# Two transformer layers in one hand-scheduled kernel: first x by tiles, another order in the opening, GpSimd's pieces ahead of its scaling, the last additions on another engine

## The reference

```python
x = x + attention(_layernorm(x), weight_qkv, weight_proj)   # 16 heads of 128, 4 groups of k and v, causal
x = x + ternary_ffn(_layernorm(x), weight, bias, gamma, beta)
x = x + linear_attention(_layernorm(x), W_in, b_in, W_out, b_out)
x = x + gated_ffn(_layernorm(x), wq_gate, s_gate, wq_up, s_up, wq_down, s_down)

# attention, the part that the opening of the change touches
scores = jnp.einsum('bsgqd,btgd->bgqst', q, k) * scale
scores = jnp.where(causal, scores, jnp.finfo(scores.dtype).min)
attn = jax.nn.softmax(scores, axis=-1)
out = jnp.einsum('bgqst,btgd->bsgqd', attn, v).reshape(b, s, NH * D)
y = jnp.einsum('bse,he->bsh', out, weight_proj)

# gated_ffn, the part that the end of the change touches
gate, up = silu(_qlinear(x, wq_gate, s_gate)), _qlinear(x, wq_up, s_up)
y = _qlinear(gate * up, wq_down, s_down)                    # W = (wq - 128) * s
```

## Time and profile before

| what | us |
|---|---|
| median of 3 runs | 589.16 (586.92 to 590.02) |
| the profiled execution | 586.79 |
| its span, first to last instruction | 584.9 |
| granted TensorE clock over the span | 0.998 of full |
| TensorE busy | 568.9 (97%) |
| VectorE, ScalarE, GpSimd busy | 477.4, 371.8, 221.4 |

### The profile page before, as it was taken

The page is one execution under the profiler, slowest core; times in us unless marked ns, Lnnn a source line. Parts: engine busy times, 40 slices in busy tenths (PEclk is TensorE's granted clock), DMA queues, the critical chain, the costliest instruction groups (busy, mean ns, idle before and its releaser), DMA issues.

```text
span 584.9 us, 12978 instructions
## 1 busy us (share of the span) xinstructions
PE 568.9 (97%) x4180; PEld 535.1 (91%) x4180; DVE 477.4 (82%) x1467; ACT 371.8 (64%) x1043; POOL 221.4 (38%) x325
## 2 busy tenths in 40 slices
PE   7999999999999999999999999999999999899995
PEld 7899999999999999999999999999998988788884
DVE  4789779778967897797789778877887989778885
ACT  5786557656765756576556657657887756554552
POOL 3666223223323332332233233323447778513220
PEclk9999999999999999999999999999999999999999
DMA  8802400000000000000000000000000000001011
GB/s 313 299 2 101 126 2 2 1 1 0 0 0 0 0 0 0 0 0 0 0 0 0 0 0 0 0 0 1 1 1 1 1 2 1 2 0 37 18 33 60
DMA packets 9136, 14.71 MB, mean 25 GB/s; under 512 B 1552, under 2 KB 6672, under 8 KB 9104
## 3 DMA queue, kind: packets, MB, share of 16 engines
q1 hardware_dynamic: 9104, 14.30, 7.0%
HBM read 12.20 MB, written 2.10 MB: 24 GB/s over the span
## 4 chain that ended last, share of the span: by engine, by line
PE 84%; DVE 7%; POOL 3%; ACT 2%; issue 2%; DMA 0%; POOLq 0%; DVEq 0%
PE bank L629 68%; PE bank L715 5%; PE bank L729 5%; PE bank L732 2%; PE bank L639 2%; PE bank L824 1%; ACT prob L1099 1%; DVE pT L1710 1%; DVE prob L1501 1%; DVE raw L1694 1%; DVE prob L1703 1%; DVE prob L1479 1%; POOL qkv L464 1%; DMA x<-in_x 0%; PE bank L893 0%
## 5 line engine op out<-in xcount | busy, mean ns | idle before, releaser
L508 POOL TENSOR_SCALAR prob<-prob,rowinv 128x128 f32<-128x128 f32 (+1 forms) x128 | 96.9, 769 | 275.5 <-DVE rowinv L1495 275.5
L629 PE MATMUL bank<-xT,big 128*128 128x256 f32 x984 | 129.3, 283 | 0.1
L629 PEld LDWEIGHTS bank<-xT,big 128*128 128x128 f32 x984 | 123.4, 192 | 1.0 <-issue 0.2
L1099 ACT ACTIVATE prob<-prob,negmax 128x128 f32<-128x128 f32 (+1 forms) x256 | 112.8, 445 | 7.8 <-DVE negmax L1479 7.8
L629 PE MATMUL bank<-wp,oT 128*128 128x256 f32 x768 | 102.3, 283 | 0.0
L629 PEld LDWEIGHTS bank<-wp,oT 128*128 128x128 f32 x768 | 96.9, 190 | 0.7
L1061 ACT ACTIVATE qT<-bank 128x512 fp32r<-128x512 f32 x68 | 40.6, 598 | 76.8 <-PE bank L629 76.8
L629 PE MATMUL bank<-pT,v 128*128 128x512 f32 (+1 forms) x384 | 79.9, 343 | 0.2
L629 PEld LDWEIGHTS bank<-pT,v 128*128 128x128 f32 x384 | 63.1, 189 | 9.9 <-issue 0.7
L1433 DVE TENSOR_TENSOR pT<-bank,pT 128x512 fp32r<-128x512 f32 (+1 forms) x128 | 65.2, 551 | 2.4 <-ACT pT L1061 2.3
L1061 ACT ACTIVATE pT<-bank 128x512 fp32r<-128x512 f32 (+1 forms) x128 | 55.2, 484 | 12.0 <-PE bank L729 9.5
(11 more groups left out here) (165 smaller groups left out, 973.0 us busy)
## 6 DMA issues: line engine op xcount, KB each, us to landing
x<-in_x SPq DMA_DIRECT2D x8, 256.0 KB, 7.9
raw<-in_wq SPq DMA_DIRECT2D x4, 512.0 KB, 8.2
raw<-in_wp SPq DMA_DIRECT2D x4, 512.0 KB, 8.2
out<-x SPq DMA_DIRECT2D x7, 256.0 KB, 2.1
raw<-in_w_gu SPq DMA_DIRECT2D x2, 640.0 KB, 5.2
raw<-in_w_in SPq DMA_DIRECT2D x1, 768.0 KB, 4.5
raw<-in_w_down SPq DMA_DIRECT2D x1, 640.0 KB, 7.1
raw<-in_wk SPq DMA_DIRECT2D x1, 512.0 KB, 3.8
```

Source lines behind the costliest of these rows:

```text
L508: m = pool.tensor_scalar(prob[:, j % 2, 0, a:b], prob[:, j % 2, 0, a:b], rowinv[:, j % 2, r:r + 1], None, ALU.mult)
L629: m = pe.matmul(out, lhs(a), rhs(b), start=first and i == 0, stop=last and i == len(passes) - 1, skip_group_check=True)
L1099: m = act.activation(prob[:, j % 2, i, a:b], prob[:, j % 2, i, a:b], ACT.Exp, scale=-1.0, bias=negmax[:, 2 * i + r:2 * i + r + 1], accum_o ...
```

## The change

The first x comes in two transfers, one for each of its tiles; VectorE takes the statistics of each tile when it lands and signals each normalised tile by itself, and TensorE transposes tile by tile. ScalarE makes the first q copy ahead of the second late chunk instead of behind it. GpSimd does its weight pieces ahead of its scaling, in the opening and in the iterations of batch 0. ScalarE and VectorE have another order in iteration 0 of batch 0, and VectorE scales ahead of the row maxima in iterations 1 to 4. At the end TensorE alternates the two halves of the last down products, and the sum for sequence 6 moves from VectorE to GpSimd.

```diff
--- before.py
+++ after.py
@@ -173,6 +173,8 @@
         s_x = [sem(f"x_landed{b}") for b in range(NB)]
+        s_x0 = [sem(f"first_x_landed{t}") for t in range(ST)]
+        s_xn0 = sem("first_xn_tile_ready")
         s_raw = [sem(f"raw_landed{c}") for c in range(10)]
         s_const = sem("constants_made")
         s_wsplit = sem("early_weights_split")
@@ -380,7 +382,8 @@
         @block.sync
         def _(sp):
-            sp.dma_start(x[:, 0:ST, :], x_v[0]).then_inc(s_x[0], 16)
+            for t in range(ST):
+                sp.dma_start(x[:, t:t + 1, :], x_v[0][:, t:t + 1]).then_inc(s_x0[t], 16)
             for n, c in enumerate(CHUNKS):
                 if n >= NRAW:
@@ -413,10 +416,10 @@
                 sp.dma_start(wd[half * HLAST:(half + 1) * HLAST, HT - 1, :], wd_in[(HT - 1) * P:HID, :]).then_inc(s_rawl[3], 16)
             for b in range(NB - 1):
-                sp.wait_ge(*((s_ga, b + 3) if b < NB - 2 else (s_gl, 1)))
+                sp.wait_ge(s_ga, b + 3)
                 sp.dma_start(out_v[b], x[:, ST * b:ST * (b + 1), :]).then_inc(s_out, 16)
             for t in range(ST):
-                sp.wait_ge(s_gl, t + 2)
+                sp.wait_ge(s_gl, t + 1)
                 sp.dma_start(out_v[NB - 1][:, t:t + 1], x[:, ST * (NB - 1) + t:ST * (NB - 1) + t + 1, :]).then_inc(s_out, 16)
             sp.wait_ge(s_out, 16 * (NB + 1))
@@ -532,6 +535,8 @@
             def batch(n, last):
                 for j in range(J):
+                    if isinstance(n, int) and n == 0 and j + 4 < len(LATE):
+                        late_lo(j + 4)
                     if j < J - 2 or not last:
                         normalise(*ahead(n, j, 2))
                     if not (isinstance(n, int) and n == 0):
@@ -553,8 +558,6 @@
                             gated_weights_lo(GU1, 0)
                     if j == J - 1 and not last and not (isinstance(n, int) and n == 0):
                         linear_scale(n - 1)
-                    if isinstance(n, int) and n == 0 and j + 4 < len(LATE):
-                        late_lo(j + 4)
             pool.wait_ge(s_var, 1)
             pool.tensor_tensor(rstd[:, :], variance[:, :], exponent[:, 0:ST], ALU.pow).then_inc(s_rs, 1)
@@ -562,8 +565,8 @@
             late_lo(1)
             late_lo(2)
             normalise(0, 0)
+            late_lo(3)
             normalise(0, 1)
-            late_lo(3)
             batch(0, False)
             pool.wait_ge(s_tab, 16 * 6)
             with pool.Fori(1, NB - 1) as n:
@@ -622,6 +625,10 @@
             with pool.Fori(1, NB // 2 - 1) as m:
                 gated(m, False, False)
             gated(NB // 2 - 1, False, True)
+            b = NB - 2
+            pool.wait_ge(s_gsc, b + 1)
+            xs = x[:, ST * b:ST * (b + 1), :]
+            pool.tensor_tensor(xs, xs, scaled[0][:, :, :], ALU.add).then_inc(s_ga, 1)
         def mm3(pe, out, lhs, rhs, first, last, passes=PASSES):
@@ -1010,7 +1017,11 @@
             pe.wait_ge(s_const, 4)
             keep_busy(20)
-            x_transpose(0)
+            for t in range(ST):
+                pe.wait_ge(s_xn0, t + 1)
+                for k in range(KT):
+                    m = pe.transpose(bY[:, k * S + t * P:k * S + (t + 1) * P], xn[:, t, k * P:(k + 1) * P], ident[:])
+            m.then_inc(s_xTp, 1)
             keep_busy(8)
             first_k()
             first_q()
@@ -1042,8 +1053,8 @@
                 with pe.Fori(1, NB // 2 - 1) as m:
                     gated(m, False, False, weight_parts)
                 gated(NB // 2 - 1, False, True, weight_parts)
-                for half in range(2):
-                    for i in (HT - 2, HT - 1):
+                for i in (HT - 2, HT - 1):
+                    for half in range(2):
                         down_project(NB // 2 - 1, i, weight_parts, half)
@@ -1108,7 +1119,11 @@
                         pT_hi(n, j)
                     if first:
                         v_hi(n, 1)
+                        late_hi(4)
                         q_hi(n, 3)
+                        o_hi(n, 0)
+                        exps(n, 2)
+                        pT_hi(n, 1)
                     if last:
                         if j == 0:
                             subtract_zero_point(GU0, 0)
@@ -1122,10 +1137,8 @@
                             subtract_zero_point(GU1, 0)
                         if j == 4:
                             gated_weights_hi(GU1, 0)
-                    if isinstance(n, int) and n == 0 and j + 4 < len(LATE):
+                    if isinstance(n, int) and n == 0 and 0 < j < len(LATE) - 4:
                         late_hi(j + 4)
-                    if first:
-                        pT_hi(n, 1)
                     if j == 1 and isinstance(n, int) and n == 0:
                         act.wait_ge(s_rawt, 16)
                         act.activation(abs_w, raw_t, ACT.Abs, accum_out=abs_sum[:, 0:1]).then_inc(s_abs, 1)
@@ -1167,9 +1180,9 @@
                             linear_k(0, 1)
                     if j == J - 1:
                         o_hi(n, j)
-                    if j < J - 3 or not last:
+                    if (j < J - 3 or not last) and not first:
                         exps(*ahead(n, j, 2))
-                    if j < J - 3 or j < J - 1 and not last:
+                    if (j < J - 3 or j < J - 1 and not last) and not first:
                         o_hi(n, j)
                 if not last:
                     v_hi(n + 1, 0)
@@ -1374,8 +1387,8 @@
             early(1, 1)
             k_hi(0, 0)
             late_hi(0)
+            q_hi(0, 0)
             late_hi(1)
-            q_hi(0, 0)
             late_hi(2)
             k_hi(0, 1)
             q_hi(0, 1)
@@ -1513,14 +1526,19 @@
                     if not (isinstance(n, int) and n == 0 and j == 1):
                         pT_lo(n, j, 0)
                         pT_lo(n, j, 1)
+                    opening = isinstance(n, int) and n == 0 and j < 5
                     if first:
                         v_lo(n, 1)
-                        q_lo(n, 3)
+                    if opening and not first:
+                        normalise(n, j + 1)
                     if j < J - 2 or not last:
                         row_max(*ahead(n, j, 2))
-                        if not first:
+                        if not opening:
                             normalise(*ahead(n, j, 1))
                     if first:
+                        q_lo(n, 3)
+                        o_lo(n, 0)
+                        invert_sums(n, 2)
                         pT_lo(n, 1, 0)
                         pT_lo(n, 1, 1)
                     if j == 0 and not first:
@@ -1845,11 +1863,21 @@
             bG, bU, bD = (bS0, bT0), (bS1, bT1), (bQ, bO)
             dve.wait_ge(s_const, 4)
-            dve.wait_ge(s_x[0], 16)
-            ln_moments(0, 0)
+            for t in range(ST):
+                dve.wait_ge(s_x0[t], 16)
+                m = dve.bn_stats(stats[:, t, :], x_tile(0, t))
+            m.then_inc(s_st, 1)
+            dve.wait_ge(s_st, 1)
+            for t in range(ST):
+                m = dve.bn_aggr(moments[:, t, :], stats[:, t, :])
+            m.then_inc(s_mo, 1)
             dve.wait_ge(s_mo, 1)
             dve.tensor_scalar(variance[:, :], moments[:, :, 1], 1.0, EPS, ALU.mult, ALU.add).then_inc(s_var, 1)
-            x_apply(0)
+            dve.wait_ge(s_rs, 1)
+            for t in range(ST):
+                dve.tensor_scalar(xn[:, t, :], x_tile(0, t), moments[:, t, 0:1], rstd[:, t:t + 1], ALU.subtract,
+                                  ALU.mult).then_inc(s_xn0, 1)
+            dve.sem_inc(s_xn, 1)
             early(0, 0)
             early(0, 1)
             x_lo(0)
@@ -1896,11 +1924,7 @@
             with dve.Fori(1, NB // 2 - 1) as m:
                 gated(m, False, False)
             gated(NB // 2 - 1, False, True)
-            b = NB - 2
-            scale_down(b, 0)
-            dve.wait_ge(s_gsc, b + 1)
-            xs = x[:, ST * b:ST * (b + 1), :]
-            dve.tensor_tensor(xs, xs, scaled[0][:, :, :], ALU.add).then_inc(s_gl, 1)
+            scale_down(NB - 2, 0)
             b = NB - 1
             dve.wait_ge(s_gd, b + 1)
             dve.wait_ge(s_ga, b + 1)
```

## The result

The median fell from 587.25 us (10 executions, 585.3 to 590.02) to **584.3 us** (10 executions, 582.26 to 584.65). The ratio is 0.9935, 95% interval [0.9915, 0.9955]: faster by 0.65%, just over what a measurement of this kernel can tell. The profiled execution took 584.11 (span 582.3) against 586.79 (span 584.9), so **2.68 us less, where the working had summed to 2.7**. What failed isn't the sum but what it was added to; that is settled further down. That the two agree to 0.02 is luck in part: the last sum ends 2.98 us earlier, and 0.4 of it is given back behind it, where the stores land (3.7 us from the last sum to the end of the span before, 4.1 after), which the working hadn't treated.

What follows compares the result with a forecast made beforehand. TensorE is busy nearly all the span, so only its waits can be won, 3.7 us in an early ScalarE, VectorE and GpSimd relay. 0.8 + 2.1 - 0.2 = 2.7 us, off the 589.16 median: 586.5, range 584.9 to 589.1.

Steps and rivals of the forecast that it cites:

- Part 1: Opening, first x by tiles: first products 0.3 us earlier, bounds 0 and 0.3, floored by dummy transposes ending at 6.24.
- Part 2: Opening, q copy ahead of a weight piece: 0.35 us carried to the second pair's exponentials, bounds 0 and 0.9.
- Rival D: Opening's wins eaten by k's late copy, TensorE 0 to 0.3 ahead at 28.50, the 2.1 stand: 587.3 us, chance 0.12.
- Part 3: Iteration 0, row maxima ahead of the q residual: scores of 28.50 come 0.8 us earlier, the carried 0.35 included.
- Part 4: Behind the scores of 28.50: VectorE's scaling and GpSimd's weight pieces no longer meet, 2.1 us of stall goes.
- Part 5: End: VectorE's first sum waits for GpSimd's 512-wide sum, 0.2 us lost, bounds -0.65 and +0.5.
- Rival C: End runs without collision and the third weight copy's data was early: 0.85 + 0.4 more won, 585.2 us, chance 0.09.
- A: Opening: VectorE's scaling meets GpSimd's piece once, 2.0 to 2.4 us lost, 588.7 us, chance 0.23.
- B: Opening: the same meeting in iterations 1 and 2 alike, 1.5 us slower, 590.7 us, chance 0.06.

Runs made afterwards that it cites:

- a_old_end: Kernel after with the end put back as it was (VectorE doing the 512-wide sum): 583.77 us, ratio 0.9925 to the kernel before.
- a_psum_end: Kernel after with VectorE's last products written to PSUM, so its last sums have one SBUF operand: 584.17 us, ratio 0.9954 to the kernel before.
- p4_both: Kernel before with GpSimd's weight pieces ahead of its scaling and VectorE's scaling ahead of the row maxima: 588.53 us, ratio 1.0013.
- p3_iteration0: Kernel before with only the new order of ScalarE and VectorE in iteration 0: 587.49 us, ratio 1.0008.
- p1_tiles: Kernel before with only the first x in two transfers and handled by tiles: 586.73 us, ratio 0.9989.
- p5_end: Kernel before with only the new end (GpSimd adds sequence 6, TensorE alternates the halves): 587.37 us, ratio 0.9996.
- p4b_vector: Kernel before with only VectorE's scaling ahead of the row maxima in iterations 1 to 4, GpSimd's order unchanged: 588.53 us, ratio 1.0012.
- b_fill: Kernel before with sixteen dummy transposes in TensorE's 1.8 us wait ahead of the gated block: 586.87 us, ratio 1.0001.
- b_xlo: Kernel before with VectorE's low part of the gated block's first x moved ahead of its last linear step: 585.79 us, ratio 0.9973.
- p4a_gpsimd: Kernel before with only GpSimd's weight pieces ahead of its scaling, VectorE's scaling still behind the row maxima: 587.55 us, ratio 1.0006.

## Why the prediction was wrong

**The anchor failed, not the sum.** The step reads: "The median of the runs shown is 589.16, 2.4 above it; against that the forecast is 586.5". The sum's own reference, 586.79, gives "584.1 for it", and the profiled execution took 584.11, the median 584.3. The three executions shown were 586.92, 589.16 and 590.02. In the 112 executions above such times as the upper two lie in the third group, that of the fallen clock, which held 34 of 112; the profiled one, with no fall in its trace, lay in the second. So I added a change worked out for the second group to a median that happened to fall in the third. With seven more executions the median is 587.25, and 587.25 - 2.7 is 584.55, within 0.3 of what came. The warning was on the table: a spread of 3.1 us among three executions, against a profile at the lowest of them.

**The sum's parts missed both ways and cancelled.** What came is 1.2 instead of 0.8 at the scores of 28.50, 1.9 instead of 2.1 behind them, -0.1 instead of -0.2 at the end, and -0.4 where the stores land, for which there was no term.

**Why the ratio says 3.8 us and the medians 2.95.** Of the ten executions beside the kernel after, three are of the third group (589.16, 589.91, 590.02), 2.0 to 2.8 us above the second group's 587.2: 0.75 us on the mean. None of the kernel after's ten is. How much of that is luck is open: of 31 executions of the kernel after and its two versions with that wait left in (a_old_end, a_psum_end) three had a clock of 0.991 to 0.994 and were over 586.5; of the kernel before about one in three. What in the change makes the falls rarer wasn't found; p4_both had more of them, not fewer: eight of its ten executions had a clock of 0.993 or less, of the kernel before 10 of 112, of p3_iteration0 two of ten.

**Part 1**: 0.17 came instead of 0.3, since the floor moved (dummy transposes to 6.59 by the timeline, not 6.24); p1_tiles showed 0.6 where the clock rose early. The bounds of 0 and 0.3 were too narrow: they held the floor fixed.

**Part 2**: I carried 0.35; alone it gave 0.56. The reason given for cutting it, that k's copy might not come earlier, fell: it came 0.19 earlier, and the third chunk's data was there. Rival D had that cause and fell with it.

**Part 3** was 0.8 at the scores of 28.50 with parts 1 and 2 in, and 1.2 came: 0.47 for the part alone (0.4 forecast), 0.57 from part 2, and the rest from part 1.

**Part 4** was 2.1 behind those scores, and 3.09 - 1.2 = 1.9 came; alone it gave 1.6. The mechanism, two engines taking turns at a port in an order set by margins of 0.1 to 0.3 us, is shown from both sides: with both halves the pairs take 0.54, with one half 2.48. Parts alone give 0.6 + 0.56 + 0.94 + 1.6 = 3.7 where the whole gave 3.1. Most of the difference is part 1, whose 0.6 came with the early clock; with the 0.17 of the kernel after they give 3.3. That the 0.2 left is parts 3 and 4 shortening the same pairs is likely and not shown.

**Part 5**: a loss of 0.2 was forecast with the sum blocked until GpSimd is done. Blocked it was. The loss is 0.1 at the last sum, in the kernel after and in p5_end alike; the median of a_old_end says 0.5, which one comparison can't tell from 0.1. Rival C's collision-free end didn't happen; its early third chunk did, and that was the smaller half of it.

**A and B** didn't happen, but only starts that lie 0.1 to 0.3 us apart separate p4b_vector, where they did, from the kernel that was measured.

## What to carry to other kernels

Anchor a sum to the same kind of execution as the profile it came from: where the executions fall into groups and a profile shows one of them, a median of three may be of another group, and the difference (here 2.4 us) can equal the change. Where two engines share a port, moving one engine's instruction moves the meeting; both orders have to be moved, and the margin between the starts read off the timeline. And fill or remove a wait of TensorE of 1 to 2 us that stands alone in a busy stretch: it may cost more than its length in some executions.

## What the runs showed of the hardware

- **The granted clock can fall behind a wait of 1.8 us**, from 1 to half (2.4 to 1.2 GHz), for 3.4 or 6.8 us, in some executions of one program and not in others. In the five profiles a fall cost 1.6 to 3.3 us at the first scaled product of the last sequences, less what the openings differ. The Trainium skill, "TensorE: Matmul & The Clock Gate", section "HAM oscillation — how this bites in real kernels", looks for this only behind longer waits; by that rule none of the falls here should have come, and the runs decide: they came behind 1.8 us, and b_fill and b_xlo had none.
- **The clock's first rise** came between 4.9 and 8.2 us into the span from one profile to the next, and the first products between 7.27 and 8.62; the latest rise has the latest products (p4a_gpsimd), but not the earliest rise the earliest (p5_end, 7.96, where TensorE waited 0.79 us for xn). An opening's gain of 0.3 us isn't to be read off one pair of profiles.
- **The last stores landed early or late.** Two stores of 128 KB each, median time from issue to landing, of b_fill and then of the kernel after:

```profile
out<-x SPq DMA_DIRECT2D x2, 128.0 KB, 1.8
```

```profile
out<-x SPq DMA_DIRECT2D x2, 128.0 KB, 3.0
```

  The landing took 1.7 to 1.8 us in three of the sixteen profiles (p4a_gpsimd, b_fill, b_xlo) and 2.4 to 3.1 in the others, and the time from the last sum to the end of the span was 2.1 to 2.2 us in those three, 3.7 in the kernel before and 4.1 in the kernel after. The distance of the first two groups of executions, 2 us, is near that size, and b_fill's and b_xlo's profiles are of the first group, the kernel before's of the second. That the landing makes these two groups is likely by this and not shown, and what sets it stayed open. By it 38 of 112 executions of the kernel before would have landed early, and one of ten of the kernel after.
- **With one operand in PSUM VectorE doesn't stand for GpSimd** (0.42 against 1.26). And VectorE's first instruction of a pair can run through where the second doesn't: of the pair of 462.68 in the earlier trace rows the first took 0.40 us, and the second, begun at 463.0, 0.82, behind GpSimd's of 462.90.
